# A graph layer whose TensorE gathers eleven batches of edges in 30 groups instead of ten, with three buffers for the kept slots and lows

## What is computed

```python
msg  = relu(x[src] + edge_attr @ We + be)                 # 200000 x 128
aggr = segment_sum(msg, dst, num_segments=6250)
h = (1 + eps) * x + aggr
h = relu(h @ W1 + b1) @ W2 + b2
h = relu(batch_norm(h) * gamma + beta) + x
out = layer_norm(x + h)
```

## Time and profile before

| | |
|---|---|
| three runs | 1581.17, 1583.06, 1585.45 us |
| median | 1583.06 us |
| span of the profiled execution, the only time the profile has for it | 2684.1 us |
| mean granted TensorE clock in it | 0.809 |
| busy in the span: PE, its weight loads, DVE, ACT, POOL | 1871.5, 1369.8, 991.5, 841.5, 1154.5 us |
| matmuls, indirect DMAs | 23395, 1145 + 31 + 3 |

### The profile page before, as it was taken

How to read it: one execution, slowest core, us unless ns; L and a number is a source line. 1 busy time by engine, 2 the same in 40 slices (tenths; PEclk the granted TensorE clock), 3 DMA queues, 4 the chain that set the end, 5 groups by cost and what they waited for, 6 DMA issues and landing times.

```text
span 2684.1 us, 58837 instructions
## 1 busy us (share of the span) xinstructions
PE 1871.5 (70%) x23395; PEld 1369.8 (51%) x23395; DVE 991.5 (37%) x3361; ACT 841.5 (31%) x1954; POOL 1154.5 (43%) x1193
## 2 busy tenths in 40 slices
PE   1776777776777777677767767767767776766776
PEld 0455555555555555555555555555555555555554
DVE  6433333333333333333333333333333333333335
ACT  3232323232332333232323323323223322322335
POOL 6444444444444444444444444434434444444421
PEclk9877788787887787788888778878778778887888
DMA  8222222232222222222222222222222222222221
GB/s 231 62 59 65 62 59 68 59 71 66 63 63 61 61 62 64 61 66 59 67 61 61 65 61 63 65 58 65 64 58 67 61 62 63 63 65 62 62 86 50
DMA packets 148455, 180.61 MB, mean 67 GB/s; under 512 B 41677, under 2 KB 128932, under 8 KB 147924
## 3 DMA queue, kind: packets, MB, share of 16 engines
q1 hardware_dynamic: 102489, 89.62, 14.0%
q0 software_dynamic: 37728, 77.31, 11.5%
q10 hardware_dynamic: 7963, 9.90, 1.2%
HBM read 170.09 MB, written 6.63 MB: 66 GB/s over the span
## 4 chain that ended last, share of the span: by engine, by line
PE 66%; issue 20%; another core or an unknown queue 8%; ACT 2%; DVE 1%; ACTq 0%; DVEq 0%
PE ps L1330 23%; PE ps L1315 15%; PE ps L1255 12%; PE ps L1269 11%; PE ps L1296 1%; PE ps L1276 1%; PE ps L1299 1%; ACT xg L694 1%; PE ps L1287 1%; PE ps L1384 1%; ACT slotS L680 0%; PE ps L1288 0%; PE ps L1394 0%; DVE lnst L1197 0%
## 5 line engine op out<-in xcount | busy, mean ns | idle before, releaser
L574 POOL DMA_INDIRECT xg<-xb,idxb x1145 | 1106.6, 966 | 1423.9 <-DVE msg L937 1068.8
L1330 PE MATMUL ps<-iota_all 128*128 128x128 bf16 x4032 | 377.8, 247 | 425.7 <-issue 291.3
L688 ACT ACTIVATE iota_all<-ps 128x384 bf16<-128x384 f32 x896 | 408.5, 489 | 775.6 <-remote 567.8
L1330 PEld LDWEIGHTS ps<-iota_all 128*128 128x128 bf16 x4032 | 290.1, 111 | 515.6 <-issue 511.5
L1022 DVE TENSOR_TENSOR accT<-accT,ps 128x64 f32 x390 | 86.5, 222 | 1138.4 <-remote 992.8
L1255 PE MATMUL ps<-we,ea 64*128 64x128 f32 x3126 | 344.2, 367 | 45.7 <-issue 45.3
L1330 PE MATMUL ps<-iota_all,hot_all 128*128 128x128 bf16 x4032 | 301.1, 229 | 102.6 <-issue 98.8
L937 DVE TENSOR_TENSOR msg<-ps,xg 128x512 f32<-128x512 f32 x390 | 262.0, 686 | 238.9 <-PE ps L1255 233.2
L1330 PEld LDWEIGHTS ps<-iota_all,hot_all 128*128 128x128 bf16 x4032 | 247.2, 102 | 172.4 <-issue 145.0
L1255 PEld LDWEIGHTS ps<-we,ea 64*128 64x128 f32 x3126 | 288.0, 261 | 80.7 <-issue 72.2
L1269 PE MATMUL ps<-msg,hot 128*64 128x128 f32 x3120 | 300.9, 352 | 6.2 <-issue 4.5
(11 more groups left out here) (135 smaller groups left out, 1113.8 us busy)
## 6 DMA issues: line engine op xcount, KB each, us to landing
ea<-in_eat SPq DMA_DIRECT2D x156, 320.0 KB
lowB<-lowD SPq DMA_DIRECT2D x128, 224.0 KB
xg<-xb,idxb POOLq DMA_INDIRECT x1145
accT<-in_xt ACTq DMA_DIRECT2D x1, 3125.0 KB
x<-in_xt ACTq DMA_DIRECT2D x1, 3125.0 KB
iota_all<-in_x ACTq DMA_DIRECT2D x1, 3080.0 KB
out<-iota_all SPq DMA_DIRECT2D x5, 512.0 KB
xb<-iota_all SPq DMA_DIRECT2D x3, 784.0 KB, 6.2
```

Source lines behind the costliest of these rows:

```text
L574: pool.indirect_dma_start(out=xg[0:rows, slot, j, :], out_offset=None, in_=of, in_offset=bass.IndirectOffsetOnAxis(ap=index, axis=0)).then ...
L688: act.activation(rows3[:, t, :, :].rearrange("p a h -> p (a h)"), ps_rows(k * NTILE + t), ACT.Copy)\
L1330: last = pe.matmul(found[:, e, :], sel2[set_of(k)][:, t, e * P:(e + 1) * P], rows3[:, t, a, :], start=(t == 0 and e == 0 and a == 0), stop ...
```

## The change

Batches are numbered through the whole loop, and their 7 steps are spread evenly: step t of batch b is in visit floor((7b + t) x 30 / 77) - 3, and the batch belongs to the group of its last step. That is eleven batches in 30 groups, 2 or 3 steps in each visit, 140 batches in all and 1563 - 3 x 140 = 1143 indirect DMAs. A visit can now hold the last steps of one batch and the first of the next; `parts` cuts its joins there, and `turn` or `count` stands between the two. `slotS` and `lowB` have three buffers (`b % 3`), so `keep_slots` of a batch waits for `select_edges` of three batches ago, not two. ACT's `take` comes ahead of `keep_slots`. `split_sources` works on all 1560 columns, not on the 390 of the batch tiles. The ring of gathered groups stays at 15, the picks' three PSUM banks too.

```diff
-    SORTED = (2, 5, 8, 11, 14, 17, 20, 23, 26, 29)
-    FIRST = tuple(3 * k - 3 for k in range(NB))
-    SHARE = tuple((3, 2, 2) if k % 2 else (2, 3, 2) for k in range(NB))
+    PER = 11
+    SKIP = 0
+    def visit_of(b, t):
+        return ((b + SKIP) * NTILE + t) * ROUND // (PER * NTILE) - 3
+    def group_of(b):
+        return visit_of(b, NTILE - 1) + 3
+    NBATCH = next(b for b in range(LOOPED) if group_of(b) > 383)
...
-        slotS = sb("slotS", [P, 2, EDGES], f16)
+        slotS = sb("slotS", [P, 3, EDGES], f16)
...
-        lowB = sb("lowB", [P, 2, NPAIR * CAP], f16)
+        lowB = sb("lowB", [P, 3, NPAIR * CAP], f16)
...
+        def parts(i, v):
+            steps = visit(i, v)
+            cut = next((m for m, (b, t) in enumerate(steps) if t == 0 and m), len(steps))
+            return steps[:cut], steps[cut:]
...
+                if b >= 3:
+                    act.wait_ge(s_sel2, b - 2)
+                act.activation(slotS[:, b % 3, :], slot_at, ACT.Copy).then_inc(s_slotS, 1)
...
-                    for j, k in phase(i, q, 3):
-                        keep_slots(j, k)
-                    for j, k in ending(i, 2 * q - 1):
-                        take(j, k)
+                    for b in ending(i, 2 * q - 1):
+                        take(b)
+                    for b in phase(i, q, 3):
+                        keep_slots(b)
...
-                source = ps[:, 3:7, :].rearrange("p a n -> p (a n)")[:, 0:LOOPED * GROUP]\
-                    .rearrange("p (m c) -> p m c", c=CYCLE)[:, :, CYCLE - HALF:CYCLE]
+                source = ps[:, 3:7, :].rearrange("p a n -> p (a n)")[:, 0:NCOL]
...
-                    for j, k, t in visit(i, 2 * q - 1):
-                        join(j, k, t)
+                    old, new = parts(i, 2 * q - 1)
+                    for b, t in old:
+                        join(b, t)
                     if not head or q:
                         turn(pair - 1)
+                    for b, t in new:
+                        join(b, t)
...
-                    for j, k, t in visit(i, 2 * q):
-                        join(j, k, t)
-                    for j, k in phase(i, q, 4):
-                        count(j, k)
+                    old, new = parts(i, 2 * q)
+                    for b, t in old:
+                        join(b, t)
+                    for b in phase(i, q, 4):
+                        count(b)
+                    for b, t in new:
+                        join(b, t)
```

More of the change, by code:

```diff
@@ L102, in gine_layer_kernel, with set_of @@
     assert NPAIR == NTILE * PAIRS and CAP * PAIRS == P
[L103 to L121, removed]
+    def visit_of(b, t):
[3 more added lines that the diff above has]
+    NBATCH = next(b for b in range(LOOPED) if group_of(b) > 383)
+    BATCH_OF = {group_of(b): b for b in range(NBATCH)}
+    VISIT = {}
+    for b in range(NBATCH):
+        for t in range(NTILE):
+            VISIT.setdefault(visit_of(b, t), []).append((b, t))
+    assert len(BATCH_OF) == NBATCH and visit_of(0, 0) // 2 - 4 >= -PRELUDE
+    def set_of(b):
+        return b % 2
     FAR = 8192.0
@@ L379, in phase, with prior, at_step @@
-        def phase(i, q, ahead):
[L381 to L386, removed]
+            return i * ROUND + g in BATCH_OF
+        def prior(b):
+            return b - 2 if b >= 2 else None
+        def at_step(b, t):
+            return b * NTILE + t
@@ L388, in visit @@
+        def phase(i, q, ahead):
+            return [b for b in range(NBATCH) if visit_of(b, 0) // 2 - ahead == i * STEPS + q]
         def visit(i, v):
-            if v < 0:
-                i, v = i - 1, v + VISITS
-            return [(i + turn, k, t) for turn, k, t in VISIT[v] if live(i + turn, k)]
+            return VISIT.get(i * VISITS + v, [])
         def ending(i, v):
-            return [(j, k) for j, k, t in visit(i, v) if t == NTILE - 1]
-        def by_pool(i, g):
-            return GROUP - HALF * special(i, g)
@@ L402, in gathered @@
[L402 to L409, removed]
+            return [b for b, t in visit(i, v) if t == NTILE - 1]
+        def parts(i, v):
+            steps = visit(i, v)
+            cut = next((m for m, (b, t) in enumerate(steps) if t == 0 and m), len(steps))
+            return steps[:cut], steps[cut:]
@@ L411, in run, with by_pool, gathered @@
+        def by_pool(n):
+            return GROUP - HALF * (n in BATCH_OF)
+        def gathered(n):
+            return 16 * sum(by_pool(m) for m in range(n % RING, n + 1, RING))
         def run(eng, iteration):
@@ L980, in ranks, with select_nodes @@
                    .then_inc(s_rel, 1)
[L982 to L984 removed]
+            def select_nodes(b):
+                old = prior(b)
                 dve.wait_ge(s_lowB, 16 * (b + 1))
@@ L1276, in turn, with count @@
                 pe.transpose(ps_turned, winS[:, :], ident[:, :]).then_inc(s_turned, 1)
-            def count(j, k):
-                b = batch(j, k)
+            def count(b):
                 pe.wait_ge(s_oh, b + 1)
-                if not isinstance(b, int) or b:
+                if b:
                     pe.wait_ge(s_slotS, b)
@@ L1289, in count, with place @@
                 last.then_inc(s_cum, 1)
-            def place(j, k):
-                b, e = batch(j, k), HALF
+            def place(b):
+                e = HALF
                 pe.wait_ge(s_rank, b + 1)
@@ L1318, in pick, with join @@
                 last.then_inc(s_st1, 1)
-            def join(j, k, t):
-                b, n = batch(j, k), at_step(j, k, t)
+            def join(b, t):
+                n = at_step(b, t)
                 pe.wait_ge(s_rows, n + 1)
```

252 lines of the change are left out of this document (112 added, 140 removed).

## The result

| | median | lowest to highest |
|---|---|---|
| before | 1584.26 us | 1581.17 to 1588.13, 4 runs |
| after | 1612.04 us | 1611.34 to 1613.44, 4 runs |

The ratio is 1.0174, with a 95% interval from 1.0159 to 1.0190: 1.7% slower, where 1611 us was forecast.

The account below looks back on a forecast made before the run. The prediction took GpSimd to end last before (ledger 1542 of 1583 us) and TensorE after: 1478, plus 77 for batches, 46 for exposed takes, 2 for split_sources and 8 for a launch, gave 1611 us, range 1556 to 1690.

Parts of the forecast that it names:

- TensorE's ledger before, 1478: TensorE's time before the change: 72 us up to the loop, 1323 for 191 pairs, 82.5 for the rest.
- remote: A 5 us wait ahead of TensorE's loop, taken off its start at 83.2 as absent in a run.
- late word: VectorE's late start on the work leading to `xb`, at 36.95 instead of about 33; 6 us off TensorE's loop start.
- A batch at 6.41 us: TensorE's work per added batch: seven steps 5.74, `place` 0.44, `count` 0.23; 77 us for 12 batches.
- The exposed take: First joins of a new batch wait for `found`, 76 places: 0.62 after turn, 0.59 after `count`, 0.83 after nothing; 46 us.
- split_sources, 2 us (0 to 6.7): Five operations ahead of the loop on 1560 columns, not 390: 2 us taken, between nothing and 6.7.
- The fifth of 41 us: Of 41 us by which GpSimd's ledger missed 1583, a fifth, 8 us, added as a launch's share.
- GpSimd at 1537 after the change: GpSimd's end by the measured median, with 36 gathers fewer, 45.6 us off.
- A: Rival: the exposed take is hidden and TensorE bounds the changed kernel, 1565 us; chance 0.13.
- B: Rival: GpSimd still bounds the changed kernel, 1537 us; chance 0.14.
- C: Rival: TensorE is bound by matmul issue, 62.3 ns each, before and after, 1681 us; chance 0.14.
- D: Rival: TensorE was already the bound by another way and its waits add up, 1706 us; chance 0.05.

## Why the prediction was right

**TensorE ends last after the change: right.** 300 us less work for GpSimd changed nothing. That 1611 came within 1 us of 1612 is luck in part: the ten batches' pairs are 5 us shorter than forecast, the takes 8 dearer, the loop starts 4.5 later, and the 8 us taken for a launch were 1.8.

**TensorE's ledger before, 1478: right,** 1479.2 with GpSimd out of the way. It hides two errors of 5 us that cancel: the loop starts at 77.3, not 72, and the loop is 5 us shorter than 1323. The start is where a step failed. I took 11 us off 83.2; in the unstretched execution before, the loop starts at 76.5, so 6.7 went. The "remote" wait of 5 us did go: from the first pick to the loop TensorE takes 8.0 us there, and took 14.1 in the stretched execution. The "late word" of 6 us didn't. VectorE began at 27.24, not 36.95, but then it waited for the stores of `xb`, four times, and the first gather from `xb` came only 0.7 us earlier than in the earlier trace rows:

```profile
45.65 2.02 DVE L1015 TENSOR_TENSOR iota_all<-iota_all,x 112x1792 f32<-112x1792 f32 x1 [2.47 <-DMA xb<-iota_all]
...
54.10 2.32 POOL L574 DMA_INDIRECT xg<-xb,idxb  x1 [2.90 <-DMA xb<-iota_all]
```

**A batch at 6.41 us: right,** 6.38. The stretches without stops of the stretched execution gave prices for picks, joins and `place` that hold to 0.01 us (0.325, 0.503 and 0.44). `count` costs 0.14, not 0.23: the joins ahead of it are 0.09 cheaper than ahead of a linear, and the 0.23 left that out. On 12 batches it is 1 us, and rounding 0.325 and 0.503 down hid most of it.

**The exposed take, 76 places and 46 us: the count was exact, the price was low.** 53.7 us by the pairs. The step that failed is the 0.62 and 0.59: they are right for the stop, and leave out that a split makes one more border between joins and picks or a linear, at 0.08 to 0.10. It could have been read from the rows before: 27 joins ahead of a linear take 1.61, ahead of `count` 82.98 - 81.46 = 1.52. The bound of 68 us held it.

**split_sources, 2 us (0 to 6.7): within the bounds, but the 2 is not shown.** Its five operations take 6.6 us on 1560 columns, not the 8.9 of five times the dearest; the first two, on VectorE:

```profile
28.25 1.78 DVE L877 TENSOR_SCALAR hot_all<-ps 128x1560 f32<-128x1560 f32 x1 [2.34 <-PE ps L1218]
30.07 0.97 DVE L878 TENSOR_SCALAR hot_all<-hot_all 128x1560 f32<-128x1560 f32 x1
```

They took 2.2 before, so VectorE has 4.4 us more to do; but behind them it waits for x's load, 4.50 us in the unstretched execution before and 0.70 in the changed kernel, and that covers all but 0.6. The loop starts at 78.51, against 76.53 before. But in the ten profiled executions here with the wide preparation (the kernel with extra matmuls left out) it starts anywhere from 76.50 to 80.27, so these 2 us can't be told from what executions differ by.

**Three buffers, nothing: right for the change, wrong as a reason.** I let DVE's and ACT's busy shares speak for it. Without the third buffer the same program is 10 us slower, so the nothing was bought by the buffer.

**The fifth of 41 us "for a launch", 8: wrong in kind, and right in size by luck.** Outside the span lie 1.8 us. The rest covered the late loop start (4.5), the tail (1.3) and what the pairs took over 1446 (2). Of the 41 us missing from GpSimd's ledger 2.0 lie outside the span; the rest are longer gathers, a longer distance, stops, and the stretch between the last gather and the last addition.

**GpSimd at 1537 after the change: not measured.** In no kernel with eleven batches does GpSimd end last. 1579 less 12 batches gives 1533. With the joins moved, the last gather ends at 1495.1, and with 45.8 and 2.0 behind it that is 1543, an estimate, since those gathers are longer. Both are below TensorE. **A, B, C and D** have each fallen by a run of their own: the moved joins (A), fewer gathers (B), 57.5 ns (C), fewer gathers and extra matmuls with ten batches (D). One sign that I had named for B, a kernel with ten batches that keeps its time beyond 0.4 us of extra work in a pair, came near to showing: of 0.447 us a pair, 87 us in all, only 10.3 were seen. It spoke of the kernel before, where TensorE had not 64 but 99.5 us to spare; what decides B in the changed kernel is the run with fewer gathers.

## What to carry to other kernels

Hold two ledgers against each other, each from stretches in which the engine never stopped; when work is moved from the engine that ends last to one that has room, the balance point is where they cross, and here the change went past it, to a TensorE ledger 31 us above GpSimd's, and then paid 49 more for an order of instructions. Near the crossing the ledgers themselves were not constant: GpSimd's gathers became longer. When steps of two batches share one accumulator and stand back to back, count the places in the program's order: the drain of the accumulator is exposed at each one, and a move of a few instructions behind other work gives it back without any change of the work. A second or third buffer's worth is read from what stands in line behind the instruction that would wait, not from how busy its engine is.

## What the hardware showed unexpectedly

A profiled execution can be unlike the ones that are timed. The first one of the kernel before took 1.70 times a run and showed GpSimd waiting 1068.8 us for VectorE; the second took 1578.1 us and showed 6.4. The single instructions and unstopped stretches were right in both, the waits only in the second.

The mean length of a gather from `xb` isn't fixed. With ten batches it is 979 to 980 ns, 986 with extra matmuls beside it, 970 with fewer gathers, and 966 in the stretched execution; with 10.75 batches 991; with eleven 985 to 989, fewer gathers or not, and 994 without the third buffer; with 10.5, in its quickest run, 978. On 1150 gathers 10 ns are 11 us, as much as was lost at the balance. Why is open.
